# Planned times of the gelu steps, the weight splits and the W1 preparation moved in a one-core AdaLN-FFN kernel

## What is computed

```python
y   = zX*lap_x(x) + zY*lap_y(x) + zR*x*(1-x)          # 1024 x 512
W1b = W1 + scale * outer(even[:4], odd[:4])            # 2048 x 512
W2b = W2 + scale * outer(even[4:], odd[4:])            # 512 x 2048
h   = gelu(y @ W1b.T + b1)
out = x + h @ W2b.T + b2
```

## Time and profile before

| | us |
|---|---|
| median of 3 runs | 1443.73 |
| the profiled execution | 1442.67 |
| its span in the profile | 1440.9 |
| PE busy (5780 matmuls) | 1341.0 |
| DVE busy | 1067.9 |
| ACT busy | 816.3 |
| POOL busy | 452.9 |

### The profile page before, as it was taken

How to read it: one execution, slowest core, us unless ns; L and a number is a source line. 1 busy time by engine, 2 the same in 40 slices (tenths; PEclk the granted TensorE clock), 3 DMA queues, 4 the chain that set the end, 5 groups by cost and what they waited for, 6 DMA issues and landing times.

```text
span 1440.9 us, 17040 instructions
## 1 busy us (share of the span) xinstructions
PE 1341.0 (93%) x5780; PEld 1091.4 (76%) x5780; DVE 1067.9 (74%) x1687; ACT 816.3 (57%) x1403; POOL 452.9 (31%) x406
## 2 busy tenths in 40 slices
PE   1398999899999999989999999999999999999999
PEld 0277788778887788767887788877888778888887
DVE  7988867778677786778767787777867787675553
ACT  2565556555576555755466554665547664566532
POOL 6454103451035501444024530255103450133000
PEclk9599999999999999999999999999999999999999
DMA  6487567966679757796588856797568865778443
GB/s 130 105 198 192 150 205 180 223 175 189 175 187 234 176 164 189 196 229 167 166 177 234 199 170 189 175 234 187 172 186 190 229 166 164 189 183 232 137 165 81
DMA packets 192679, 262.56 MB, mean 182 GB/s; under 512 B 20432, under 2 KB 94160, under 8 KB 192592
## 3 DMA queue, kind: packets, MB, share of 16 engines
q1 hardware_dynamic: 174928, 211.15, 49.4%
q0 software_dynamic: 17664, 50.34, 20.5%
HBM read 194.19 MB, written 67.24 MB: 181 GB/s over the span
## 4 chain that ended last, share of the span: by engine, by line
PE 68%; DVE 17%; ACT 5%; issue 5%; DMA 5%; POOL 0%; SPq 0%; DVEq 0%; ACTq 0%
PE po L389 12%; PE po L390 12%; PE po L391 12%; PE ph L372 11%; PE ph L376 10%; PE ph L374 10%; DVE W2s L357 4%; DMA EB<-ep_scratch 4%; DVE y L248 2%; DVE W1l L319 2%; DVE y L250 2%; DVE y L249 1%; DVE W2l L364 1%; ACT R L303 1%; DVE ph L422 1%
## 5 line engine op out<-in xcount | busy, mean ns | idle before, releaser
L372 PE MATMUL ph<-yh,W1h 128*128 128x512 f32 x896 | 359.8, 402 | 69.9 <-ACT UVs L425 28.4
L389 PE MATMUL po<-W2h,gh 128*128 128x512 f32 x1024 | 400.2, 391 | 0.0
L390 PE MATMUL po<-W2l,gh 128*128 128x512 f32 x1024 | 399.8, 390 | 0.0
L391 PE MATMUL po<-W2h,gl 128*128 128x512 f32 x1024 | 399.4, 390 | 0.0
L407 DVE TENSOR_TENSOR gl<-ph,gh 128x512 fp32r<-128x512 f32 x256 | 176.1, 688 | 257.4 <-ACT gh L405 257.1
L374 PE MATMUL ph<-yl,W1h 128*128 128x512 f32 x896 | 354.5, 396 | 0.0
L376 PE MATMUL ph<-yh,W1l 128*128 128x512 f32 x896 | 354.3, 395 | 0.0
L402 ACT ACTIVATE ph<-ph,b1t 128x512 f32<-128x512 f32 x256 | 169.3, 661 | 251.0 <-DVE ph L453 80.9
L372 PEld LDWEIGHTS ph<-yh,W1h 128*128 128x128 f32 x896 | 170.9, 191 | 125.8 <-ACT UVs L425 35.9
L357 DVE SCALAR_TENSOR_TENSOR W2s<-EB,SC,W2s 128x128 f32<-128x128 f32 x512 | 218.3, 472 | 18.7 <-DMA EB<-ep_scratch 18.1
L116 POOL DMA_DIRECT2D R<-in_w_dram x64 | 56.3, 880 | 546.1 <-ACT R L303 532.0
(11 more groups left out here) (73 smaller groups left out, 1256.6 us busy)
## 6 DMA issues: line engine op xcount, KB each, us to landing
R<-in_w_dram POOLq DMA_DIRECT2D x64, 512.0 KB, 7.7
W2s<-in_w_dram SPq DMA_DIRECT2D x128, 256.0 KB, 4.9
uv_scratch<-UVs SPq DMA_DIRECT2D x128, 256.0 KB, 3.1
UVs<-uv_scratch SPq DMA_DIRECT2D x128, 256.0 KB, 3.0
X<-in_xT_dram SPq DMA_DIRECT2D x58, 390.0 KB, 5.3
td_scratch<-Ts SPq DMA_DIRECT2D x64, 256.0 KB, 4.0
xr<-in_x_dram SPq DMA_DIRECT2D x16, 1024.0 KB, 8.7
xr<-in_b_dram POOLq DMA_DIRECT2D x16, 1024.0 KB, 10.6
```

The lines of the kernel that those rows point to most:

```text
L372: e.matmul(bank[:, :], W1h[:, f, blk, wc], yh[:, s, c, :], start=first and c == 0, stop=False, skip_group_check=not first)
L389: e.matmul(po[t][:, :], gh[:, late, st], W2h[:, k, :], start=first, stop=False)
L390: e.matmul(po[t][:, :], gh[:, late, st], W2l[:, k, :], start=False, stop=False)
L391: mm = e.matmul(po[t][:, :], gl[:, late, st], W2h[:, k, :], start=False, stop=last)
```

## The change

Only planned times change, so the same instructions stand in another order on ACT, DVE, POOL and SP. The order of PE is the same, row for row. The gelu of the first tile of a first-half pair moves from T+16 to T+23, behind the copy L425 at T+21; its low part from T+33 to T+37. The second tile's steps and those of the second half move by 0.5 to 4 units. The high part of W2 moves 5 units back and its low part 7. For W1 the load of `EB1`, the four outer-product pieces and the accumulating load move back by 8 to 10 units (4 for pair 2), and the two low parts by 3.

```diff
--- before.py
+++ after.py
@@ -287,8 +287,8 @@
         def w1_pair(b, i):
             T, f, j = t0(b, 0, i), i % 2, i // 2
             ahead = (-134, -90, -80) if b == 0 and i == 1 else (-134, -110, -100) if i == 1 else \
-                (-150, -122, -112) if i == 2 else (-172, -130, -118)
-            w = [T + a for a in (*ahead, -50, -43, -39, -30, -45, -39, -29.5, -24)] if b or i else \
+                (-150, -118, -108) if i == 2 else (-162, -120, -110)
+            w = [T + a for a in (*ahead, -50, -43, -39, -30, -45, -36, -29.5, -21)] if b or i else \
                 [us(a) for a in (14, 18, 20, 25, 26.5, 27.5, 29, 24.6, 25.5, 28.2, 29)]
             back = outer.at(b, i - 1) if i else outer.at(b - 1, 7)
             k = d_e1.dma(sp, w[0], [(EB1[:, :], EP[8 * b + j:8 * b + j + 1,
@@ -359,9 +359,9 @@
                     W2s[:, s, 128 * a:128 * a + 128], ALU.mult, ALU.add), kd, k_e2[b, jk], scal.at(b))
             w2fold[b, n] = m
             done = l2E if k % 2 == 0 else l2L
-            m = act.put(when + 8, lambda e: e.activation(W2h[:, k, :], W2s[:, s, :], ACT.Copy), m,
+            m = act.put(when + 13, lambda e: e.activation(W2h[:, k, :], W2s[:, s, :], ACT.Copy), m,
                         done.at(b - 1, 1, k // 2))
-            w2lo[b, n] = dve.put(when + 12, lambda e: e.tensor_tensor(
+            w2lo[b, n] = dve.put(when + 19, lambda e: e.tensor_tensor(
                 W2l[:, k, :], W2s[:, s, :], W2h[:, k, :].bitcast(f32), ALU.subtract), m)
 
 
@@ -432,8 +432,8 @@
                                 ytile.at(0, 4) if b == 0 else None)
             stV[b, i] = d_us[1].dma(sp, T + 39, [(UV[i, 1], UVs[:, 2, :])], cpV.at(b, i), ldV.at(b - 1, i))
             m = p3[b, i] = product(T + 48, X, f, 1, yh0, yl0, 4, False, loB.at(b, i), opd.at(b, 4), cpV.at(b, i))
-            gelu(b, 0, i, 0, Y, (T + 16, T + 30, T + 33), c11.at(b, i))
-            gelu(b, 0, i, 1, X, (T + 54, T + 57, T + 60), p3.at(b, i))
+            gelu(b, 0, i, 0, Y, (T + 23, T + 30.5, T + 37), c11.at(b, i))
+            gelu(b, 0, i, 1, X, (T + 55, T + 58, T + 64), p3.at(b, i))
 
         def half1(b, i):
             T = t0(b, 1, i)
@@ -452,8 +452,8 @@
             m = p4[b, i] = product(T + 18, Z, f, o + 1, yh1, yl1, 1, False, loQ.at(b, i), opd.at(b, 6), c22.at(b, i))
             c21[b, i] = dve.put(T + 24, lambda e: e.tensor_tensor(Z[:, :], Z[:, :], UVs[:, su, :], ALU.add),
                                 m, ldU.at(b, i))
-            gelu(b, 1, i, 0, Q, (T + 9, T + 18, T + 20.7), c22.at(b, i))
-            gelu(b, 1, i, 1, Z, (T + 27, T + 36, T + 39), c21.at(b, i))
+            gelu(b, 1, i, 0, Q, (T + 11, T + 18.5, T + 23), c22.at(b, i))
+            gelu(b, 1, i, 1, Z, (T + 29, T + 36.5, T + 41), c21.at(b, i))
 
         def l2_of(b, h, i, T, h_next):
             spots = (12, 21, 24, 27) if h_next == 0 else (6, 9, 12, 15)
```

## The result

The changed kernel takes 1426.37 us (median of 4 runs, 1420.55 to 1427.07) against 1443.74 of the kernel before: a ratio of 0.987, 95% interval [0.9845, 0.9897]. It is faster, but by 17 us where 48.5 were forecast, and outside the range given.

A forecast was written before the change was run, and what follows sets the result against it. The prediction took PE's own work plus its waits for ACT copies to bound the kernel. Terms 35.0 + 8.0 + 3.5 + 2.0 = 48.5 us off 1442.67 gave 1394.2, shown as a median of 1395, range 1383 to 1420.

The forecast's parts named there:

- What bounds the kernel: Whole kernel: PE is busy 1341.0 of 1440.9 us; apart from the start it waits only on ACT copies L425 and L430.
- L425 and L430 in images 1 to 6: First halves of images 1 to 6: PE's waits for both copies go, 37.4 us recoverable, 35.0 us counted.
- What is late next is L430 in pair 3: Pair 3, images 1 to 6: L430 ends 0.2 us before PE wants it; 0.4 us per image left, 2.4 us.
- Clock: Images 1 to 6: five half-clock stretches after longer PE waits go with those waits, 1.6 us each, 8.0 us.
- Terms one and two: Images 1 to 6: the L425 and L430 waits, 35.0 us, and the half-clock stretches, 8.0 us.
- Image 0 after its first pair: Image 0: L425 waits mostly stay behind W2's high part; moving the gelu away gains 3.5 us, bounds 0 and 9.7.
- Start: PE's first waits, for L418 and L425: an operand split ahead of the row load's wait, and the gelu gone, gain 2.0 us.
- the wait moves: Rival, chance 0.17: PE's wait moves from p5 to p3, DVE bounding pairs 3 and 4; gain 22 us, 1422 us.
- The fold that meets POOL: Pairs 3 and 4: one more DVE fold meeting a POOL instruction delays DVE 1.57 us in twelve places, about 19 us less gain.

The follow-up runs named there:

- e10: The changed kernel with the W2 folds of the first part of a pair planned 7 units later in image 0: 1418.3 us, ratio 0.982.
- e5: The changed kernel without the loads of X for images 1 to 7, whose stencils read what X holds from image 0: 1405.9 us, ratio 0.973.
- e16_both: The changed kernel with b2's first-half load behind the last stencil tiles and image 0's W2 folds 7 units later: 1400.6 us, ratio 0.970.
- e6_b2_later: The changed kernel with the 1 MB accumulating load of b2 of each first half planned 43 units later: 1441.3 us, ratio 0.997.
- e9_b2_last: The changed kernel with b2's accumulating load of each first half planned at +402 units instead of +170, behind the last stencil tile's X load: 1407.5 us, ratio 0.974.
- e14_before_no_x: The kernel before the change without the loads of X for images 1 to 7: 1449.1 us, ratio 1.003.

## Why the prediction was wrong

**What bounds the kernel: right.** PE's own work and its waits, of which those for ACT's copies are the largest in all the kernels run.

**L425 and L430 in images 1 to 6, 35.0 us: the waits went, the gain didn't.** 33.7 us of brackets became 2.5, as forecast, and no wait for L430 came in pair 3 of image 3, whose margin was forecast as 0.2 us: it ended at 623.47 (622.88 + 0.59), and p3 began at 623.57. The step that failed is "What is late next is L430 in pair 3 ... I leave 0.4 us per image". What was late next was L418 of pair 4, 2.6 to 3.2 us in each image. The text looked for the next late instruction among those that the diff moves, up to the end of the same pair. L246 and the load of `X` aren't in the diff, but they had only 1.4 us to spare, and the change shortened their cover by 2.7. Of the 35.0 us 13.4 came: 37.4 less the new waits, 21.6 us in 15 waits with 0.16 each.

**Clock, 8.0 us: mostly not.** The step took the stretches to go with the waits. The waits came back with the same size, and with them the stretches. After the wait above, in columns of the earlier trace rows:

```profile
628.00:630.00 2.00, 0.59 (x3) 0.17 (x1) 1.01 (x2) 0.45 (x2) 0.20 (x1) 1.00 1.08 390
632.00:634.00 2.00, 2.00 (x6) 1.52 (x6) 2.00 (x3) 0.00 (x0) 2.00 (x3) 0.50 0.15 33
```

Half clock again behind an idle PE. Images 1 to 6 now have four stretches of 3.4 us at half clock (from 293.1, 631.0, 801.7 and 1139.6 us) where they had five, so by the forecast's own 1.6 us a stretch some 1.6 came of 8.0. All loss outside the waits, 35.8 - 21.6 - 15 x 0.16 = 11.8 us, was 52.6 - 33.7 - 3.7 = 15.2 before: 3.4 less, of which 1.8 has no name. Terms one and two together: 43 forecast, 16.8 measured.

**Image 0 after its first pair, 3.5 us: -3.2.** Its loss there rose from 14.0 to 17.3 us. The reason given for a small gain, that L362 stays ahead of L425, was right, and it did more than that: with the gelu gone from before it, ACT only waited longer for the same folds. e10 shows that the folds' place was worth 8 us in the whole image.

**Start, 2.0 us: 2.7.** PE's three waits in pair 0 lost 15.0 us and lose 13.3, so 1.7 came as forecast. Another 1.0 came from the clock, which the forecast had left out there: it was back at full speed at 67.8 us, before at 74.2. The measured terms, 16.8 - 3.2 + 2.7, make 16.3 us; the span is 16.0 us shorter.

**The rival "the wait moves", 1422 us at 0.17,** had the time nearly and the mechanism not: it expected DVE as the bound in pair 3, where 1.60 us before the late DVE row are idle. Its argument from sums (11.33 of 12.50 us busy) could not tell a full engine from one that waits for a load.

**The fold that meets POOL** (about 19 us less gain) came, but is not what took the 26 us. A fold took 540 ns in the mean, 472 before, 34 us more DVE work over the run. But at the new wait ACT stood for `X` and DVE was idle, and in e5, where a fold takes 581 ns, 20 us came all the same.

**What remains of the old price.** The forecast took a measured wait as the gain of removing it. In pairs 1 and 3 that held, 26.4 us of loss went there; 13.4 came back in pair 4. b2's transfer costs either order some 19 us, over different paths: in the old one partly by POOL and DVE to L425 in pair 3, in the new one by the late `X` to L418. Its issue stands among the very rows in which the forecast found the slow folds (623.60 to 625.20), and was passed over. With the two edits of e16_both images 1 to 6 gain 35.0 us, of the 43.0 forecast for them.

## What to carry to other kernels

A profile puts a wait down to the instruction that was waited for, not to what made that one late. Before pricing its removal, follow every in-order queue for a whole period, past the instructions that the change moves, and ask of each load how much cover it has left once PE is that much earlier. Look for the slowest instance of each repeated transfer and for what runs beside it: a median of 5.3 us hid six of 9, and moving what ran beside them was worth 19 us. And where several orders lose the same time at different instructions, look for what they wait on before moving more of them, and compare the times: a wait that ended before the suspect landed has another cause.

## What the runs showed of the hardware

A 1 MB accumulating load issued by POOL landed 11.8 us after its issue (10.5 in the other order), and the 390 KB load issued 3.1 to 4.2 us behind it took 7.8 to 10.4 us (before, after and e6_b2_later), where it takes 5.4 to 5.5 in image 3 without it (e9_b2_last and e6_b2_later). Issued 0.6 us behind it, in images 3 to 6 of e9_b2_last, it took 5.9 to 7.5 us three times and 13.7 us once, and the 1 MB load 13.4 to 14.7.

From 617 to 629 us, with the 1 MB load under way, the DMA engines were busy for 0.98 of the time and moved 214 GB/s; from 628 to 630, as it ended, they moved 390 GB/s at a share of 1.08. The busy share doesn't say how much passes.

A DVE subtraction of 128x1024 took 5.09 us beside five POOL sums in a row (e14_before_no_x), 1.21 in the kernel before.
